# Table parts subtracted on TensorE, biases in the table, and one measurement for two normalizations, in a four-layer graph network

## What is computed

```python
# layer 0: two graph convolutions; layers 1 to 3: attention over the edges
x = LN(x + gcn(x))
x = LN(x + L1(x))     # L1: prelu(LN(attend(x @ W) + bias) * ln_w + ln_b), 4 heads
x = LN(x + L2(x))     # L2: elu(attend(x @ W)) + x @ W_res, 8 heads
x = LN(x + L3(x))
# L3: h = attend(LN(x, ln1_g, ln1_b) @ W) + gat_b + x ; h + ffn(LN(h, ln2_g, ln2_b))
# attend: xh = h @ W;  alpha = leaky_relu(a_src[src] + a_dst[dst]); softmax over the edges of a target;
#         out[dst] = sum alpha * xh[src];   L1 and L3 add an edge from each node to itself
```

## Time and profile before

| | us |
|---|---|
| median of 3 runs (4275.5 to 4282.44) | 4278.55 |
| the profiled execution | 4277.48 |
| its span, first to last instruction | 4275.7 |

### The profile page before, as it was taken

The page is one execution under the profiler, slowest core; times in us unless marked ns, Lnnn a source line. Parts: engine busy times, 40 slices in busy tenths (PEclk is TensorE's granted clock), DMA queues, the critical chain, the costliest instruction groups (busy, mean ns, idle before and its releaser), DMA issues. The chain is left out here.

```text
span 4275.7 us, 61386 instructions
## 1 busy us (share of the span) xinstructions
PE 2828.8 (66%) x16208; PEld 1819.7 (43%) x16208; DVE 3116.2 (73%) x9331; ACT 2391.8 (56%) x5229; POOL 2872.2 (67%) x3193
## 2 busy tenths in 40 slices
PE   1698888994567676676256776767625666676763
PEld 1344444552345444454234444535423444454542
DVE  5999997555467777678747786877874777686785
ACT  0677775003556666664356665656545666665644
POOL 5799994202777777773477777777437777777743
PEclk8899999996788888897578887888867888897886
DMA  3011111451232333231133333233103323232220
GB/s 102 28 82 81 58 78 81 167 216 47 64 69 68 69 68 69 69 69 43 32 69 70 70 70 70 66 70 70 41 22 73 69 68 69 69 69 68 64 51 15
DMA packets 127618, 298.41 MB, mean 70 GB/s; under 512 B 45412, under 2 KB 74972, under 8 KB 123712
## 3 DMA queue, kind: packets, MB, share of 16 engines
q0 software_dynamic: 74976, 155.58, 16.6%
q1 hardware_dynamic: 52320, 139.24, 9.7%
HBM read 241.28 MB, written 53.38 MB: 69 GB/s over the span
## 5 line engine op out<-in xcount | busy, mean ns | idle before, releaser
L1411 POOL DMA_INDIRECT work<-table,lane_src x2184 | 2092.5, 958 | 665.6 <-issue 643.7
L1508 PE MATMUL psum<-work 128*128 128x396 bf16 (+1 forms) x5850 | 1165.0, 355 | 68.1 <-ACT work L1453 34.4
L1450 ACT ACTIVATE work<-work,middle_node_number 128x384 f16<-128x384 f16 x1587 | 954.3, 601 | 225.1 <-PE psum L1508 202.8
L1453 ACT ACTIVATE work<-work 128x384 bf16<-128x384 f16 x1587 | 829.6, 523 | 50.5
L1565 PE MATMUL psum<-work 128*128 128x136 f32 x4836 | 701.2, 304 | 188.9 <-DVE work L1696 96.5
L1508 PEld LDWEIGHTS psum<-work 128*128 128x128 bf16 x5850 | 598.2, 104 | 513.8 <-issue 122.5
L1565 PEld LDWEIGHTS psum<-work 128*128 128x128 f32 x4836 | 654.6, 209 | 273.7 <-issue 160.6
L1733 DVE TENSOR_TENSOR node_sums<-node_sums,psum 128x136 f32 x2418 | 558.1, 293 | 103.1 <-PE psum L1565 96.2
L767 POOL TENSOR_SCALAR work<-work 128x128 f16<-128x128 f16 x784 | 540.7, 708 | 74.9 <-POOLq L663 60.2
L745 DVE TENSOR_SCALAR work<-work 128x400 f16<-128x400 f16 x1568 | 484.9, 351 | 6.4 <-PEq L663 3.6
L716 PE MATMUL psum<-work 128*128 128x448 f16 x2100 | 456.1, 355 | 3.2 <-PEq L1131 2.5
(11 more groups left out here) (361 smaller groups left out, 2852.8 us busy)
## 6 DMA issues: line engine op xcount, KB each, us to landing
counts<-work SPq DMA_DIRECT2D x14, 2800.0 KB, 9.3
work<-counts SPq DMA_DIRECT2D x14, 2800.0 KB, 10.2
work<-table,lane_src POOLq DMA_INDIRECT x2184, 2.6
work<-spread SPq DMA_DIRECT2D x78, 256.0 KB, 4.0
work<-masks SPq DMA_DIRECT2D x78, 128.0 KB, 3.0
work<-source_rows SPq DMA_DIRECT2D x39, 192.0 KB, 3.8
spread<-node_sums SPq DMA_DIRECT2D x4, 896.0 KB
table<-work SPq DMA_DIRECT2D x10, 330.0 KB, 3.0
```

The source lines that it names most:

```text
L1411: pool.indirect_dma_start(m.ring[:, s % SLOTS, 0:F + H], None, m.d_table[H], bass.IndirectOffsetOnAxis(ap=m.src[:, s:s + 1], axis=0)).then ...
L1450: act.activation(away, rows_of(g, u), ACT.Abs, bias=m.low_tile[:, hi:hi + 1]).then_inc(far_known, 1)
L1453: act.activation(hot_of(g, u), away, ACT.Relu, bias=1.0, scale=-1.0).then_inc(hot_act, 1)
L1508: mm = pe.matmul(aid_banks[:, k, 0:3 * (F + H)], hot_of(g, u)[:, k * P:(k + 1) * P], m.all_thirds[:, :, hi, 0:F + H], start=(hi == 0), sto ...
```

## The change

1. **Subtraction on PE.** `rest` and `lowest` are gone from DVE. Instead PE repeats the block's product from its stationary copy and adds to it, in the same accumulation, a product of a minus identity (bf16, made once in `extend_weights` by a new DVE operation) with the high part (first repetition), then with the high and the middle part (second repetition). ACT copies middle and low from PSUM. Repetitions of block b - 1 and b - 2 stand on PE between the turning and the product of block b; ACT's copies of middle (block c - 1) and low (block c - 2) stand between its copy of the turned tiles and its wait for the product. The turned copies are three in turn instead of two.
2. **Two biases in the table.** In the first and third node stage each product is followed by a product of one row of ones with the bias, in the same accumulation (columns 0 to 127 alone); so are the repetitions. The bias additions of `divided` in the second stage and in the last stage are gone.
3. **One measurement for two normalizations.** In the third stage the steps are three instead of five. From the first measurement DVE works out also the variance of the normalized rows, ACT takes both roots in one operation, and ACT writes both normalized outputs from the same input (`act_normal_pair`, ten activations in a row).

The diff, cut to its core:

```diff
@@ extend_weights
+    chain(dve.tensor_scalar(m.minus_ident[:], m.ident[:], -1.0, None, ALU.mult))
@@ new functions
+def measure_pair(dve, chain, m, b, x):
...
+    plain, second = m.mean_var[:, j, 1:2], m.var_pair[:, j, 1:2]
+    chain(dve.tensor_scalar(m.var_pair[:, j, 0:1], plain, 1e-5, None, ALU.add))
+    chain(dve.reciprocal(m.inv_pair[:, j, 0:1], m.var_pair[:, j, 0:1]))
+    chain(dve.tensor_tensor(second, plain, m.inv_pair[:, j, 0:1], ALU.mult))
+    chain(dve.tensor_scalar(second, second, 1e-5, None, ALU.add))
+    chain(dve.reciprocal(m.inv_pair[:, j, 1:2], second))
+def refine_pair(dve, chain, m, b):
...
+def act_normal_pair(act, m, b, x, out, again):
+    for k in range(BLK):
+        t = b * BLK + k
+        act.activation(out[:, k, :], x[:, k, :], ACT.Identity, bias=m.root_pair[:, t, 0:1], scale=m.inv_pair[:, t, 0:1])
+    for k in range(BLK):
+        t = b * BLK + k
+        last = act.activation(again[:, k, :], x[:, k, :], ACT.Identity, bias=m.root_pair[:, t, 1:2], scale=m.inv_pair[:, t, 1:2])
+    return last
@@ node_stage, vector
-            def rest(b):
-            def lowest(b):
...
-                if 0 <= b < TURNS:
-                    if self_loops:
-                        scores(b)
-                    rest(b)
-                if b >= 1:
-                    lowest(b - 1)
-            dve.wait_ge(thirds_known, len(parts) * TURNS)
+                if self_loops and 0 <= b < TURNS:
+                    scores(b)
@@ node_stage, tensor
+            def product(b, k, less):
+                t = pe.matmul(out(b, k), turned_sb[b % 3][:, k * P:(k + 1) * P], w_ext[:], start=True, stop=bias is None and not less)
+                if bias is not None:
+                    t = pe.matmul(out(b, k)[:, 0:F], over(m.ident[0:1, 0:1], [1, P]), m.weights[bias][0:1, 0:F], start=False, stop=not less)
+                for third in less:
+                    t = pe.matmul(out(b, k)[:, 0:F + H], m.minus_ident[:], third[:, b * BLK + k, :], start=False, stop=third is less[-1])
+                return t
+
+            def remainder(b, less, taken, known):
+                for n, (lo, hi) in enumerate(parts):
+                    pe.wait_ge(taken, len(parts) * b + n + 1)
+                    for k in range(lo, hi):
+                        t = product(b, k, less)
+                    t.then_inc(known, 1)
...
                 t.then_inc(turned, 1)
+                if b:
+                    remainder(b - 1, (high,), high_taken, rest_known)
+                if b >= 2:
+                    remainder(b - 2, (high, middle), middle_taken, low_known)
                 pe.wait_ge(copied, b + 1)
                 if b >= 2:
                     pe.wait_ge(thirds_known, len(parts) * (b - 1))
...
                 for k in range(BLK):
-                    t = pe.matmul(out(b, k), lhs[k], w_ext[:], start=True, stop=True)
+                    t = product(b, k, ())
...
+            remainder(TURNS - 2, (high, middle), middle_taken, low_known)
+            remainder(TURNS - 1, (high,), high_taken, rest_known)
+            remainder(TURNS - 1, (high, middle), middle_taken, low_known)
@@ node_stage, scalar (middles and lows are copies of PSUM to a bf16 part)
+                if c:
+                    middles(c - 1)
+                if c >= 2:
+                    lows(c - 2)
                 act.wait_ge(multiplied, c + 1)
...
-                if c:
-                    middles(c - 1)
...
+            lows(TURNS - 2)
             middles(TURNS - 1)
+            lows(TURNS - 1)
+            act.wait_ge(thirds_known, len(parts) * TURNS)
@@ first_stage
-    node_stage(nc, m, 4, m.weights["L1_ext"], m.x, (measured, refined), (rooted, normal))
+    node_stage(nc, m, 4, m.weights["L1_ext"], m.x, (measured, refined), (rooted, normal), bias="L1_gnn_bias")
@@ second_stage
-        chain(dve.tensor_tensor(o[:, j, :], o[:, j, :], block_row(m, "L1_gnn_bias"), ALU.add))
@@ third_stage
-    node_stage(nc, m, 4, w["L3_ext"], t, (divided, rectified, refined, measured, refined), (exponent, rooted, normal, rooted, normal_again),
-               merge=merge, affine=(w["L3_gnn_ln1_g"], w["L3_gnn_ln1_b"]))
+    node_stage(nc, m, 4, w["L3_ext"], t, (divided, rectified, refined), (exponent, rooted, normal),
+               merge=merge, affine=(w["L3_gnn_ln1_g"], w["L3_gnn_ln1_b"]), bias="L3_gnn_gat_b")
@@ last_stage
-                chain(dve.tensor_tensor(o_b, o_b, block_row(m, "L3_gnn_gat_b"), ALU.add))
```

More of the change, by code:

```diff
@@ L1865, in node_stage @@
     wide = F + 2 * H
[L1866 removed]
+    turned_sb = [m.big[:, q * cols:(q + 1) * cols] for q in range(3)]
     parts = ((0, 3), (3, BLK))
     last = len(steps) - 1
[L1869 removed]
+    ph, (turned, copied, multiplied, residual, tables, spread_known, stored, high_taken, rest_known, middle_taken, low_known, thirds_known, merged,
          residual_taken, pool_step, dve_step) = phase(
         nc, "tiles_turned", "turned_copied", "product_done", "residual_done", "table_copied", "spread_known", "table_stored", "high_taken",
[L1872 removed]
+        "rest_known", "middle_taken", "low_known", "thirds_known", "sums_merged", "residual_taken", "pool_step", "dve_step")
     high, middle, low = (third[:, :, 0:F + H] for third in m.thirds)
@@ L1904, in scores @@
                 dve.engine_nop().then_inc(spread_known, 1)
-            def rest(b):
[L1907 to L1911, removed]
-            def lowest(b):
[L1914 to L1919, removed]
+            for wave in range(TURNS + last + 2):
                 for i, step in enumerate(steps):
@@ L1952, in _ @@
                     pe.wait_ge(thirds_known, len(parts) * (b - 1))
-                lhs = [turned_sb[b % 2][:, k * P:(k + 1) * P] for k in range(BLK)]
+                lhs = [turned_sb[b % 3][:, k * P:(k + 1) * P] for k in range(BLK)]
                 for k in range(BLK):
-                    t = pe.matmul(out(b, k), lhs[k], w_ext[:], start=True, stop=True)
+                    t = product(b, k, ())
                 t.then_inc(multiplied, 1)
@@ L1962, in _, with copies, lows @@
                     t.then_inc(residual, 1)
+            remainder(TURNS - 2, (high, middle), middle_taken, low_known)
+            remainder(TURNS - 1, (high,), high_taken, rest_known)
+            remainder(TURNS - 1, (high, middle), middle_taken, low_known)
         @block.scalar
         def _(act):
+            def copies(b, third, known, taken):
+                for n, (lo, hi) in enumerate(parts):
+                    act.wait_ge(known, len(parts) * b + n + 1)
+                    act.copy(third[:, b * BLK + lo:b * BLK + hi, :], out_part(b, n)[:, :, 0:F + H]).then_inc(taken, 1)
             def middles(b):
[L1967 to L1970, removed]
+                copies(b, middle, rest_known, middle_taken)
+            def lows(b):
+                copies(b, low, low_known, thirds_known)
             for wave in range(TURNS + last + 1):
@@ L1984, in _ @@
                 if affine is None:
-                    act.copy(turned_sb[c % 2], m.ps[0][:, 0:cols]).then_inc(copied, 1)
+                    act.copy(turned_sb[c % 3], m.ps[0][:, 0:cols]).then_inc(copied, 1)
                 else:
                     gain, shift = affine
-                    act.activation(turned_sb[c % 2], m.ps[0][:, 0:cols], ACT.Identity, bias=shift[:, 0:1], scale=gain[:, 0:1]).then_inc(copied, 1)
+                    act.activation(turned_sb[c % 3], m.ps[0][:, 0:cols], ACT.Identity, bias=shift[:, 0:1], scale=gain[:, 0:1]).then_inc(copied, 1)
+                if c:
+                    middles(c - 1)
+                if c >= 2:
+                    lows(c - 2)
                 act.wait_ge(multiplied, c + 1)
```

39 lines of the change are left out of this document (30 added, 9 removed).

## The result

| | median us | runs | lowest to highest |
|---|---|---|---|
| before | 4277.03 | 4 | 4275.5 to 4282.44 |
| after | 4424.72 | 4 | 4423.79 to 4425.49 |

The ratio is 1.0349, 95% interval 1.0336 to 1.0362: slower by 148 us, where +21.6 was forecast. The profiled execution took 4424.91 us, span 4423.1.

The account below looks back on a forecast made before the run. POOL gathers without pause in an attention, so a later first gather ends it later. Stage terms +18.0, +8.2, -1.0 and -3.6 sum to +21.6 on 4278.55: 4300 us, 8-in-10 range 4281 to 4335.

Parts of the forecast that it names:

- the rival of the slow clock: PE stays at 1.2 GHz in all the new turns: +117 us, 4395; chance 0.14 for anything from 4316 up.
- Three points a stage: Each node stage priced at first table copy, its spacing over five blocks, and hand-over to the attention; last stage by its chain.
- DVE's relief worth nothing: First stage: removing `rest` and `lowest` from DVE gives nothing, since DVE waits in this stretch.
- PE setting the turns of the first stage: First stage, one product's end to the next: PE's repetitions and product make 11.0 us; ACT's own sum is 6.4.
- the hand-over bound by low copies: First stage, last table copy to first gather: low parts bind instead of scatters, 10.9 us instead of 9.5, +1.4.
- 1st stage: First node stage: longer turns, slow first product's bias and later low parts, +18.0 us.
- 2nd: Second node stage: bias additions gone before the first table, turns +4.5 us longer, net -1.0 us.
- 3rd: Third node stage: first table copy -11.5 us, turns +18.3, hand-over +1.4, net +8.2 us.
- last: Last stage, ending the program: bias additions saved on DVE, -3.6 us, taken between bounds of 2.6 and 5.1.
- the first product's bias: First stage, before the first table copy: bias on the first, slow product costs +2.15 us.
- PE's prices: PE, five tiles, fast (slow): product with bias 2.7 (4.8), first repetition 3.05 (5.8), second 3.35 (6.4) us.
- Granted clock above 0.8 in the turns: Sign expected in the changed trace: PE's granted clock exceeds 0.8 between table copies; 0.60 was granted before.

Follow-up runs that it names:

- full rows: Changed kernel with the bias product made through the identity and the bias on all 128 rows instead of one: 4288.60 us, ratio 1.0032 to the kernel before.
- The shared measurement alone: Kernel before with only the third stage's one measurement for two normalizations added: 4275.61 us, ratio 0.9983.
- the one-row bias alone: Kernel before with the two biases put on the table by one-row products, no repetitions, the two additions gone: 4321.15 us beside 4281.79.

## Why the prediction was right or wrong

**Right side, wrong size.** Slower was given 0.76; the time lies 90 us above the range, and above the rival of the slow clock (4395) too. The side isn't luck: the forecast loss came from the bias products, and with full rows they do make the kernel slower by 13.6 us, while without them it isn't told from the kernel before.

**The structure held.** Three points a stage, DVE's relief worth nothing (with subtraction on PE and no bias the first gather of the first stage starts at 1061.86 us, before at 1061.56), PE setting the turns of the first stage, the hand-over bound by low copies with POOL waiting: all are in the rows. The third stage differs in one point: its two middle turns were forecast as ACT's, 11.6 us, and with full rows they are 10.6 us, as in the first stage. With full rows the terms can be read at their own prices:

| | forecast | full rows |
|---|---|---|
| 1st stage | +18.0 | +13.4 |
| 2nd | -1.0 | -4.1 |
| 3rd | +8.2 | +6.2 |
| last | -3.6 | -2.6 |
| all, by the medians | +21.6 | +13.6 |

A turn of 10.6 against 11.0 and a hand-over of 10.5 against 10.9 are good. Of the rest, the first product's bias (+2.15) didn't show (-0.1), though that point moved by -1.8 and +1.5 us in the two kernels with the shared measurement, which leave the first stage as it was; and the second stage's turns took 32.8 us where I had 36.5, the first 8.9 us instead of 10.2, the last two 7.7 and 7.5 us instead of 8.9 and 8.5.

**The step that failed is the price of the one-row bias product in "PE's prices"**: "Its bounds are next to nothing and the full 1.28; I take the full one, since it streams the same 128 fp32 columns as its nearest row." Columns were the wrong measure. Its bounds were no bounds: the rows of before show no weight with another number of rows among those of 128, so nothing showed what a change of rows does, and the upper end should have held a load that runs beside no product, and the slow clock. By the rows of the changed kernel a tile is 1.47 us where the forecast had 0.54 (fast) or 0.96 (slow). The Trainium skill page that I weighed, TensorE: Matmul & The Clock Gate, "LDWEIGHTS", is about the duration of the load, and that holds here: 0.50 us for two with one row and with 128. The Trainium skill's TensorEngine Tiling (Array Packing), which states the drain, I had not drawn on.

**The clock.** The rival of the slow clock had 0.14 and its reason against was that the change adds activity. More activity there is, by the rows, but the clock didn't rise with it: PE is 99% busy, and 66 products in 20 us are 3.3 a us where 70 in 33 us were 2.1 before, yet the clock is 0.50 where it was 0.60. It was also priced too low, at 18.9 us a turn instead of 25.2, since it kept the loads beside the products. "Granted clock above 0.8 in the turns" is refuted for the kernel and true with full rows. What would have shown it wrong was written down, "over 15 (slow clock)", and it is what came.

**Third stage.** First table copy 11.5 us earlier by the forecast. It came 9.1 us earlier after the start of the stage, with a bias product 2.6 us dearer than assumed (7.4 against 4.8) in it: -11.7 without that. The shared measurement alone gives -13.9 with no bias product. The turns of that kernel, 37.4 us against 29.4, show the cost that was foreseen of ten activations in a row.

**Second stage.** The first table copy stands 5.1 us nearer to the start of the stage; forecast -5.9.

**Last stage.** -3.8 against -3.6, in which there is some luck: the twelve other kernels without that addition range from -1.2 (96 and 127 rows) to -3.8. The long additions did move partly: the median of the next addition went from 0.825 us to 1.769, its longest from 2.041 to 2.121. In the first three blocks the removed additions had taken 5.0 us, and the next additions became 2.3 us longer, which leaves 2.7. That is close to the 2.6 of the rule by which the next addition takes over the wait (the Trainium skill, GPSIMD Engine Reference, "Specifications", as in the prediction), though no run shows the shared interface itself. The other 1.1 us are not explained, nor why two kernels with next additions of the same length won only 1.2.

```profile
L2239 DVE TENSOR_TENSOR work<-work,node_x x5: 824/1769/2121, 4326.7 to 4365.4; 128x640 f32<-128x640 f32 x5
```

**Open.** Why the clock falls. It fell with one row and with 64, with the loads apart and with most of them beside products, with PE 73% and 99% busy, and it stayed at 1.00 with one small product a block; what lies between one and five was not tried. The number of products doesn't settle it: the one-row bias alone begins 125 in 59 us of the first stage, the kernel before 70 in 33, the same 2.1 a us, at clock 0.50 and 0.60. Whether the clock falls by the changes of rows themselves, or because with loads standing apart the array streams for less of the time than the busy share says, no run separates. Weights of fewer than 128 columns, and stretches of one-row products alone, were not tried either.

## What to carry to other kernels

Keep the number of rows of the weights the same within a stream of products: make a bias product through an identity and the bias on all rows (128 were measured, and 96 and 127 took as long), and read the idle time of the weight loads ("<-issue") wherever the number of rows changes. Where no row of a trace shows a form of instruction beside its neighbours, its cost is not bounded by its own columns; the upper bound has to hold the overlap and the clock that the stream around it loses. And put work that nothing in the stage waits for into the wait of its engine, not in front of what the others need.

## What the runs showed of the hardware that I had not expected

- A weight of one row between weights of 128: the load starts 0.07 us before the recorded end of the product before it, with 128 rows 0.28 us before. A tile is 0.84 us instead of 0.46 at 2.4 GHz, 1.47 instead of 0.88 at 1.2 GHz. Weights of 64 rows give the same turn as one row (25.2 us), weights of 96 and 127 rows that of 128 (10.65 against 10.6).
- The granted clock falls to 0.50 while such products follow each other, with PE busy for 99% of a stretch of 20 us; products of 128 rows of the same length, 86% busy, keep 1.00.
- Cutting the 15 one-row products of a turn from 128 to 2 columns wins only 3.1 us of the 14.6 that full rows win: 0.2 us each.
